# Packing a loop's three run-time numbers into one register value

## The reference

```python
xn = _layernorm(x, axis=-1)                       # 625 x 512
hp = xn @ weight
agg = segment_sum(hp[src] * edge_weight[:, None], dst, num_segments=625)
x = x + relu(agg) + mix(xn)
```

## Time and profile before

| | |
|---|---|
| median of 3 runs | 1158.62 us (1157.82 to 1162.06) |
| the profiled execution, its own time | 1158.62 us |
| its span in the profile | 1157.0 us |
| PE busy | 1096.4 us, 95% |
| DVE busy | 558.1 us, 48% |
| the window loop | from 45.2 us to 123.0 us of the span |

### The profile page before, as it was taken

The page is one execution under the profiler, slowest core; times in us unless marked ns, Lnnn a source line. Parts: engine busy times, 40 slices in busy tenths (PEclk is TensorE's granted clock), DMA queues, the critical chain, the costliest instruction groups (busy, mean ns, idle before and its releaser), DMA issues.

```text
span 1157.0 us, 20011 instructions
## 1 busy us (share of the span) xinstructions
PE 1096.4 (95%) x7329; PEld 738.9 (64%) x7330; DVE 558.1 (48%) x1388; ACT 370.1 (32%) x931; POOL 139.5 (12%) x192
## 2 busy tenths in 40 slices
PE   3899999999999789999998899999999999999998
PEld 2588646467776564455544477878477878755664
DVE  7999738645545421011110444544233455587641
ACT  1112212045555311222212345554114455412530
POOL 1045460020000420101101440000000000002000
PEclk9999999999999769999999999999999999999999
DMA  4100475001000479700799750100210100010001
GB/s 131 37 1 3 130 196 209 1 28 29 29 1 1 163 272 390 294 16 18 284 409 399 276 196 29 29 8 22 73 55 28 29 28 1 1 36 1 1 1 44
DMA packets 19098, 112.69 MB, mean 97 GB/s; under 512 B 4871, under 2 KB 6648, under 8 KB 14942
## 3 DMA queue, kind: packets, MB, share of 16 engines
q1 hardware_dynamic: 13560, 100.95, 23.3%
q0 software_dynamic: 5472, 10.83, 3.6%
HBM read 102.78 MB, written 8.98 MB: 97 GB/s over the span
## 4 chain that ended last, share of the span: by engine, by line
PE 85%; DMA 5%; DVE 5%; issue 2%; ACT 2%; SPq 0%; DVEq 0%; ACTq 0%
PE psum L611 11%; PE psum L794 10%; PE psum L978 7%; PE psum L959 6%; PE psum L817 6%; PE psum L679 6%; PE psum L848 5%; PE psum L799 5%; PE psum L830 5%; DMA arena<-in_moe_b 5%; PE psum L1098 3%; PE psum L1003 3%; PE psum L1076 3%; PE psum L629 3%; PE psum L751 2%
## 5 line engine op out<-in xcount | busy, mean ns | idle before, releaser
L611 PE MATMUL psum<-arena 128*125 128x512 f32 x320 | 143.2, 604 | 2.6 <-DVE arena L1612 1.9
L1200 ACT ACTIVATE arena<-arena,small 125x625 f32<-125x625 f32 x120 | 97.0, 809 | 89.9 <-DVE small L1592 89.9
L794 PE MATMUL psum<-arena 128*128 128x313 f32 (+1 forms) x384 | 111.7, 440 | 2.8 <-ACT arena L1139 1.9
L611 PEld LDWEIGHTS psum<-arena 128*125 128x125 f32 x320 | 60.5, 192 | 77.4 <-issue 71.9
L1275 ACT ACTIVATE arena<-psum,cols 128x64 f32<-128x64 f32 x224 | 47.5, 361 | 188.7 <-PE psum L965 188.7
L978 PE MATMUL psum<-arena 128*64 128x256 f32 x896 | 101.2, 384 | 5.7 <-DMA arena<-in_moe_b 3.7
L959 PE MATMUL psum<-arena 128*64 128x512 f32 x448 | 99.8, 598 | 4.0 <-DMA arena<-in_moeW 3.7
L794 PEld LDWEIGHTS psum<-arena 128*128 128x128 f32 x384 | 70.9, 192 | 32.1 <-issue 3.4
L1592 DVE CUSTOM_DVE_ANT_0 arena<-psum,cnt_adj 125x625 f32<-125x625 f32 x80 | 61.5, 806 | 57.4 <-PE psum L817 57.4
L978 PEld LDWEIGHTS psum<-arena 128*64 128x64 f32 x896 | 64.1, 138 | 39.0 <-ACT arena L1275 7.1
L1208 ACT ACTIVATE arena<-psum 125x500 f32<-125x500 f32 x120 | 63.8, 583 | 73.2 <-PE psum L830 73.2
(11 more groups left out here) (298 smaller groups left out, 1440.8 us busy)
## 6 DMA issues: line engine op xcount, KB each, us to landing
arena<-in_moeW SPq DMA_DIRECT2D x16, 4096.0 KB, 19.0
arena<-in_att SPq DMA_DIRECT2D x36, 256.0 KB, 2.8
arena<-in_l1W SPq DMA_DIRECT2D x2, 2048.0 KB, 10.2
token_rows<-arena POOLq DMA_DIRECT2D x19, 128.0 KB, 5.0
rows<-in_rows SPq DMA_DIRECT2D x1, 2240.0 KB
expert_rows<-arena POOLq DMA_DIRECT2D x17, 128.0 KB, 4.8
arena<-in_gnnWo SPq DMA_DIRECT2D x2, 1024.0 KB, 6.1
arena<-token_rows POOLq DMA_DIRECT2D x14, 128.0 KB, 7.1
```

What stands on the lines that cost most here:

```text
L611: mm = pe.matmul(bank(b, NP, D), srcT[:, k, c * NP:(c + 1) * NP], w[:, k, :], start=(k == 0), stop=(k == KC - 1))
L794: mm = pe.matmul(bank(b, P, width), aw[:, w, k, :], srcT[:, k, o:o + width], start=(k == 0), stop=(k == KC - 1))
L1200: act.activation(Sx[u % 3][h], Sx[u % 3][h], ACT.Exp, bias=small[0:NP, 80 + n:81 + n], scale=-1.0, accum_out=small[0:NP, 120 + n:121 + n]) ...
```

## The change

The three numbers that a window needs, its first tile, its number of groups and the number of groups before it, are put into one integer: groups in the lowest 6 bits, first tile in the next 8, groups before it above. DVE forms that integer in floating point with two operations in place of three; one matmul in place of two turns the column into a row; each engine loads 20 registers in one load in place of 40 in two. Ahead of each window's loop the queue takes the number apart again with shifts and masks (`tile_range`). The loop now counts groups from 0, and the tile's number and the value to wait for are worked out with a multiplication by six in each group.

```diff
         def window_ranges(engine):
-            first, second = [nc.values_load_multi_w_load_instructions(
-                bounds[0:1, o:o + NW], engines=[engine], min_val=-NW * KG * GT, max_val=NW * KG * GT,
-                skip_runtime_bounds_check_because="the program clamps a window's first tile and its count")[1]
-                for o in (0, NW)]
-            return [0] + list(first), second
+            _, values = nc.values_load_multi_w_load_instructions(bounds[0:1, 0:NW], engines=[engine], min_val=1,
+                                                                 max_val=NW * KG * 16384 + 64 * ET + KG)
+            return values
+
+        def tile_range(eng, packed):
+            return (eng.snap((packed >> 6) & 255, min_val=0, max_val=ET - 1), eng.snap(packed & 63, min_val=1, max_val=KG),
+                    eng.snap(packed >> 14, min_val=0, max_val=(NW - 1) * KG))
...
-            for v in range(2):
-                mm = pe.matmul(bank(4, 1, WMIN - NW * v, NW * v), w_cols[:, 2 + v:3 + v], ident[0:NW, 0:WMIN - NW * v],
-                               start=True, stop=True)
-            mm.then_inc(range_rows, 1)
+            pe.matmul(bank(4, 1, WMIN), w_cols[:, 2:3], ident[0:NW, 0:WMIN],
+                      start=True, stop=True).then_inc(range_rows, 1)
...
-            ends, shifts = window_ranges(mybir.EngineType.PE)
+            ranges = window_ranges(mybir.EngineType.PE)
...
             for w in range(NW):
+                first, k, before = tile_range(pe, ranges[w])
...
-                with pe.Fori(ends[w], ends[w + 1], GT) as n:
+                with pe.Fori(0, k) as j:
                     for s in range(GT):
-                        e = nc.s_assert_within(n + shifts[w] + s, 0, TP - 1,
+                        e = nc.s_assert_within(first + j * GT + s, 0, TP - 1,
...
-                        pe.wait_ge(hot_ready, n + s + 1)
+                        pe.wait_ge(hot_ready, (before + j) * GT + s + 1)
...
-            ve.tensor_scalar(w_cols[:, 1:2], n_i[:, 1:2], float(GT), None, ALU.mult)
+            ve.scalar_tensor_tensor(w_cols[:, 1:2], w_cols[:, 0:1], 64.0, n_i[:, 1:2], ALU.mult,
+                                    ALU.add)
             norm_apply(0, xres, N1)
             ve.wait_ge(range_cum, 1)
-            ve.scalar_tensor_tensor(w_cols[:, 2:3], bank(5, NW, 1), float(GT), w_cols[:, 1:2], ALU.mult, ALU.add)
-            ve.scalar_tensor_tensor(w_cols[:, 3:4], bank(5, NW, 1), float(-GT), w_cols[:, 0:1], ALU.mult,
+            ve.scalar_tensor_tensor(w_cols[:, 2:3], bank(5, NW, 1), 16384.0, w_cols[:, 1:2], ALU.mult,
                                     ALU.add).then_inc(range_cols, 1)
```

More of the change, by code:

```diff
@@ L216, in build @@
         w_end = take(NW, 8)
-        w_cols = take(NW, 4)
+        w_cols = take(NW, 3)
         w_loops = take(NW, WMIN)
@@ L1478, in _ @@
             ve.wait_ge(range_ready, 1)
-            ends, shifts = window_ranges(mybir.EngineType.DVE)
+            ranges = window_ranges(mybir.EngineType.DVE)
             for w in range(NW):
-                with ve.Fori(ends[w], ends[w + 1], GT) as n:
+                first, k, before = tile_range(ve, ranges[w])
+                with ve.Fori(0, k) as j:
                     for s in range(GT):
-                        e = nc.s_assert_within(n + shifts[w] + s, 0, TP - 1,
+                        e = nc.s_assert_within(first + j * GT + s, 0, TP - 1,
                                                skip_runtime_bounds_check_because="a window's tiles end below TP")
-                        ve.wait_ge(hot_free, n + s + 1)
+                        ve.wait_ge(hot_free, (before + j) * GT + s + 1)
                         ve.tensor_scalar(one_src[:, s, :], iota_src[:, 0:SW], float(1024 * w), key[:, bass.ds(e, 1)],
```

## The result

| | before | after |
|---|---|---|
| median of 6 runs each | 1158.22 us (1155.57 to 1162.06) | 1171.29 us (1165.75 to 1172.35) |
| ratio | | 1.0107, 95% interval 1.0086 to 1.0128 |
| span of the profiled execution | 1157.0 us | 1170.0 us |
| opening matmuls of the first window start at | 45.24 us | 43.32 us |
| tiles' matmuls, first start to last end | 46.19 to 122.9, 76.7 us | 44.79 to 132.65, 87.9 us |

The kernel became 13.1 us slower, 1.1%. 1159.9 us was forecast, in a range up to 1164.4, and slower by over 0.5% had a chance of 0.10.

The account below looks back on a forecast made before the run. PE, busy 1096.4 of 1157.0 us, was taken to bound the kernel; in the loop DVE mostly set the pace. With 2.3 us lost in the loop and 1.0 gained ahead, 1158.6 + 1.3 = 1159.9 us, range 1157.2 to 1164.4.

Parts of the forecast that it names:

- Each window costs each queue 0.4 more: Ahead of each window's loop: the unpacking was to cost each queue 0.4 us (0.1 to 0.7).
- are about 0.05: In each group of the loop: four more operations were to cost about 0.05 us (0.02 to 0.15).
- The formula: Window of k groups: DVE takes 1.76k + 0.57 us, PE's queue 1.95(k - 1) + 1.81 plus the added costs.
- the ring: Window loop: six slots holding 1.76 us of DVE's work absorb some 0.5 us once, in windows of three groups.
- PE's queue becomes the bound: Rival, in every window: 0.7 us a window and 0.15 a group, 11.2 lost, 0.7 gained, 1169.1 us; chance 0.10.
- Windows of one group: Ten windows in the loop: PE's queue takes 2.26 us against DVE's 2.33, so nothing is lost.
- The head: Up to the first window's opening: line 669 starts at 44.2 instead of 45.24, 1.0 us gained (0.7 to 1.3).
- (a): Line 650: one transpose in place of two brings `hp` and its last copy about 0.2 us earlier, at 43.65.
- (d): Before line 1469: one tiny DVE operation less; line 1475 ends at 43.0 rather than 43.1, gaining nothing.
- (b): Before line 669: one load frees PE's queue at 40.0; 1.38 us of "issue" vanish but for what comes new.
- Everything behind the loop moves along: After the window loop: work is untouched and only shifts in time with the loop's end.
- The code's place: Rival, in the loop: 17 jumps back each lose another 0.15 to 0.2 us, 3 us more, 1163; chance 0.05.

Follow-up runs that it names:

- both_once: The changed kernel with both queues working out a window's three numbers once per window and keeping them in registers; 1167.94 us, ratio 1.0046 to the kernel before.
- four_ops: The kernel before with four more register instructions on PE's queue ahead of each window; 1163.20 us, ratio 1.0022.
- eight_ops: The kernel before with eight more register instructions on PE's queue ahead of each window; 1170.82 us, ratio 1.0105.
- after_again: The changed kernel, unaltered, measured in another session; 1171.91 us, ratio 1.0111 to the kernel before.
- no_check: The changed kernel without the 20 run-time checks of bounds on each queue; 1170.11 us, ratio 1.0063 to the kernel before.

## Why the prediction was wrong

**The step that failed is the price list of the loop**: "Each window costs each queue 0.4 more", and of a group's four more operations that they "are about 0.05". In the changed kernel a window costs nothing and a group 0.47 us on PE's queue. The formula into which these numbers went held. With 0.47 a group and nothing a window, PE takes 1.95(k - 1) + 1.81 + 0.47k: 2.28 for one group, still under DVE's 2.33, so nothing lost (measured 0.03); 4.70 for two against DVE's 4.09, 0.61 lost (0.70); 7.12 for three against 5.85, 1.27 lost, less 0.25 for the ring (1.21); 3.3 in the first window (3.7, of which 1.0 is the open 0.2 us a group). Together 9.6 (with 0.61 times seven and twice 1.27 less 0.5), where the loop grew by 11.1 (76.75 to 87.86). The forecast used the same lines and came to 2.3.

**Where the instructions stand** I took from the text of the program, in which `tile_range` is ahead of the loop. Nothing in the trace of before could tell it. But the earlier trace rows had a hint: the loop of before works out each tile's address in a fused instruction of its own, so address expressions were built where they are used. I asked what the unpacking costs and not how often it is done. The rival "PE's queue becomes the bound" had the right engine and 0.15 a group; its total of 1169.1 was near 1171.3 for other reasons, since it put 0.7 on each window.

**The size of an unpacking.** Lower end 0.1 and upper 0.7 were named for it, and 0.4 taken, on the ground that copies are dropped. `both_once` shows 0.63 a window and 0.07 a group. At those prices the formula gives 2.51, 4.53 and 6.55 for one, two and three groups, measured 2.60, 4.61 and 6.38. The copies are instructions too, and I had not counted the division. The start-to-start price of 0.1 us for a lone operation, against the 32 ns that are shown, was right (0.10 in `four_ops` and `eight_ops`). So was the choice to go by starts.

**Windows of one group** keep their length (2.37 against 2.34), but not for the reason given, that DVE's 2.33 still covers PE's queue. In the trace of after DVE waits for PE's matmuls in eight of the nine windows between 108 and 130 us, 2.5 us in all, and in those of before between 100 and 120 us not once. PE's queue sets the pace there too; it just happens to need about what DVE needed. `both_once` (2.60) and `eight_ops` (2.71) show how near that is: a little more and ten windows pay.

**The head.** Forecast 1.0 us gained up to line 669, measured 1.9 in the first profile; but `hp`'s last copy ended at 42.36 there. In `after_again` it ended at 43.76, next to the 43.85 of before, and that comparison is the clean one: 1.3 us gained to the opening (43.90), 0.8 to the first tile's matmul (45.37 against 46.19). The 0.5 between them is the unpacking behind the opening on both queues. Steps (a), one transpose less, and (d) can't be told apart from the scatter of the head. Step (b) was right in that "issue" went, though "one load of some 4.8 us" was wrong: it took 1.55, and 5.6 us of checks followed, which I had overlooked in the diff, where an argument is dropped. They cost nothing, because `hp`'s last copy and DVE's one-hot end later. That the two errors nearly cancelled (the queue is through at 41.1, forecast 40.0) was luck.

**Everything behind the loop moves along**: right within the 3.5 us by which executions of one program differ there.

**The code's place**: a taken branch itself shows 207 to 250 ns against 220 to 238 before. But the 0.2 us that five jumps back of the first window lose behind the branch, and that `no_check` with less code ahead doesn't, are what that rival described, at its price of 0.15 to 0.2 and for 5 of 17 jumps. The Trainium skill's rule that stood with it (Runtime: NRT & Kernel Launch, section Instruction fetch mechanics) speaks of a wait for the jump's target to be fetched; whether such a wait lies behind these 0.2 us no run here shows.

## What to carry to other kernels

A value that is derived from a register in the program's text may be worked out where it is used, each time; before packing run-time numbers, look in the listing or in the trace for how often the unpacking runs, and count it on the queue that sets the pace, from start to start: here 0.1 us for a lone instruction and 0.2 for a fused one that shows 150 ns. When two engines seem to wait for each other and the weight loads show "issue", suspect the queue of one of them, and move its work in one queue at a time: the queue that sets the pace answers, the other doesn't. Here 0.47 us in each of 37 turns of a loop outweighed a load that is done once, the more as most of that load lay beside other work.

## What the runs showed of the hardware

- A load of 20 registers takes 1.36 to 1.62 us when its address is a multiple of 16 bytes and 4.49 to 4.93 when it is 4 bytes behind one. It was seen in both kernels and on both queues; other distances were not tried.
- A shift to the right by 14 appears as a division in a fused instruction: 146 to 161 ns in the median on PE's queue where those in its place without it show 43 to 56. But fused instructions without a division can take as long: 146 ns for a check of bounds, 143 to 153 for the first tile's address. What in them costs the time is not shown. The Trainium skill (Perfetto Trace Analysis, section Per-instruction lifecycle) says that the profiler reports only the execution of what the sequencer handles alone. These runs agree for lone operations (32 to 36 ns shown, 0.10 us paid); for the long fused ones most of the price is in the duration that is shown (156 ns shown, 0.21 us to the next start).
- A check of one value's bounds at run time takes 0.28 us on PE's queue: a fused instruction of 146 ns and an assertion of 18 ns, with the gaps between them.
- The granted clock in the first 10 us of the loop was 0.67 to 1.00 in executions of nearly the same head; at 0.67 the first window took 1.4 us more than the model has for it.
